# Router's first product in eight array tiles with two banks, and a first-layer product issued ahead of the turned result

## The reference, cut to what matters

```
h  = h + attention(layernorm(h))
x  = layernorm(h)                                   # 64 values a token
rh = relu(x @ router_w1 + router_b1)                # 64 -> 32
g  = softmax(rh @ router_w2 + router_b2)            # 32 -> 6, then the two best
h1 = relu(x @ expert_w1[e] + expert_b1[e])          # for each of the 6 experts
h2 = relu(h1 @ expert_w2[e] + expert_b2[e])
y  = sum over the two best e of weight_e * (h2 @ expert_w3[e] + expert_b3[e])
out = h + y
```

## Time and profile before

| | us |
|---|---|
| median of 3 runs | 247.37 |
| lowest, highest | 247.05, 250.84 |
| the profiled execution, as timed | 249.88 |
| its span in the trace | 248.1 |
| TensorE busy in it | 211.6 (85%) |
| VectorE busy | 159.6 (64%) |
| ScalarE busy | 106.6 (43%) |

### The profile page before, as it was taken

How to read it: one execution, slowest core, us unless ns; L and a number is a source line. 1 busy time by engine, 2 the same in 40 slices (tenths; PEclk the granted TensorE clock), 3 DMA queues, 4 the chain that set the end, 5 groups by cost and what they waited for, 6 DMA issues and landing times.

```text
span 248.1 us, 5974 instructions
## 1 busy us (share of the span) xinstructions
PE 211.6 (85%) x2394; PEld 88.3 (36%) x2398; DVE 159.6 (64%) x331; ACT 106.6 (43%) x188; POOL 77.8 (31%) x122
## 2 busy tenths in 40 slices
PE   0477876699899989998986889999999999998892
PEld 0354533034433433334542424434342523232210
DVE  3424673236795794798379498879889785928161
ACT  1228631123353353351245346555655555454530
POOL 4000465243352263303554307170625323201010
PEclk9999999569979988999999999999999999999997
DMA  7632399999698689710010669677663919384751
GB/s 144 147 121 53 81 223 239 262 264 260 178 260 209 174 225 262 194 68 18 3 42 4 168 154 213 137 161 162 164 156 103 210 53 242 77 215 104 180 132 42
DMA packets 26282, 37.85 MB, mean 153 GB/s; under 512 B 15888, under 2 KB 17104, under 8 KB 26256
## 3 DMA queue, kind: packets, MB, share of 16 engines
q1 hardware_dynamic: 19376, 19.92, 33.6%
q0 software_dynamic: 5216, 16.98, 26.4%
q10 hardware_dynamic: 1664, 0.58, 1.2%
HBM read 17.79 MB, written 2.83 MB: 83 GB/s over the span
## 4 chain that ended last, share of the span: by engine, by line
PE 60%; DVE 13%; DMA 9%; issue 9%; ACT 5%; POOL 2%; POOLq 1%; SPq 0%; DVEq 0%; ACTq 0%
PE PS L662 11%; PE PS L686 10%; PE PS L826 8%; PE PS L815 7%; PE PS L800 7%; DMA G<-Gs 5%; PE PS L746 3%; DVE Htab L954 2%; PE PS L698 2%; PE PS L837 2%; DMA WB<-gate_scratch 2%; ACT OT L566 2%; DMA cst<-consts 2%; PE PS L610 1%; PE PS L757 1%
## 5 line engine op out<-in xcount | busy, mean ns | idle before, releaser
L229 POOL DMA_DIRECT2D G<-Gs x64 | 33.6, 530 | 63.1 <-ACT Gs L472 56.8
L662 PE MATMUL PS<-A,BD 32*32 32x256 f32 x1024 | 35.8, 410 | 9.7 <-ACT Gs L472 6.4
L1071 DVE SCALAR_TENSOR_TENSOR H2g<-PS,nb_s,WB 128x1024 f32<-128x1024 f32 x24 | 30.8, 1283 | 13.6 <-PE PS L815 10.9
L488 ACT ACTIVATE H<-PS,b_s 128x512 f32<-128x512 f32 x48 | 30.2, 679 | 11.8 <-PE PS L800 11.8
L998 DVE COPY Gs<-PS 128x512 f32<-128x512 f32 x32 | 20.9, 686 | 21.0 <-PE PS L662 12.0
L686 PE MATMUL PS<-G,cnt 128*64 128x512 f32 x128 | 33.6, 662 | 0.0
L472 ACT ACTIVATE Gs<-PS 128x512 f32<-128x512 f32 x32 | 17.6, 595 | 33.3 <-PE PS L662 29.4
L400 POOL TENSOR_TENSOR GP<-GG,GP 32x512 fp32r<-32x512 f32 x8 | 10.2, 1269 | 66.2 <-ACT GP L504 66.2
L800 PE MATMUL PS<-X,W1s 64*128 64x512 f32 x96 | 27.1, 641 | 1.3 <-ACT H L488 1.3
L815 PE MATMUL PS<-H,W2s 64*64 64x512 f32 x192 | 26.1, 614 | 1.5 <-DVE H2g L1071 1.5
L826 PE MATMUL PS<-H2g,W3s 128*64 128x512 f32 x96 | 25.7, 616 | 0.9 <-DVE Y L1132 0.5
(11 more groups left out here) (114 smaller groups left out, 289.1 us busy)
## 6 DMA issues: line engine op xcount, KB each, us to landing
G<-Gs POOLq DMA_DIRECT2D x64, 256.0 KB, 6.5
WB<-gate_scratch SPq DMA_DIRECT2D x48, 256.0 KB, 5.3
xb<-ids_scratch SPq DMA_DIRECT2D x8, 256.0 KB, 3.8
h_out<-Y SPq DMA_DIRECT2D x8, 256.0 KB, 2.7
GG<-gate_scratch SPq DMA_DIRECT2D x64, 12.0 KB
vo_scratch<-VOs SPq DMA_DIRECT2D x2, 256.0 KB, 2.1
VOr<-vo_scratch SPq DMA_DIRECT2D x4, 128.0 KB, 3.1
wk_s<-wk SPq DMA_DIRECT2D x2, 128.0 KB, 5.0
```

What stands on the lines that cost most here:

```text
L229: eng.dma_start(G2[half % G2_RING][first::8, :, :], Gs[n % GS_RING][:, m, :]).then_inc(sent[n % GS_RING][m], 16)
L488: ins = act.activation(H1[q][:, u * HT:(u + 1) * HT], PS[:, B_L1 + u, :], ACT.Relu, bias=b1_s[:, u, q:q + 1])
L662: ins = pe.matmul(PS[32 * x:32 * x + 32, B_G + i, w * NV:(w + 1) * NV], BD[n % BD_RING][rows, x].rearrange("p c f -> p (c f)")[:, w::2], A ...
L1071: dve.scalar_tensor_tensor(out=H2g[q][:], in0=two_banks(l2_bank(q)), scalar=nb2_s[:, q:q + 1], in1=WB[s % RING][:, q, :], op0=ALU.max, op1 ...
```

## The change

Two things are changed. First, `hidden` makes its product in eight matmuls of 128 tokens in place of four of 256: one for each of the four 32-column groups and each of the two halves of partitions, the halves writing to the two banks `B_X` and `B_X + 1`. `hidden_out` reads both banks (as many values as before), and the order of the sequences that comes out makes the view in `rank_experts` a plain one.

```diff
                 for j in range(4):
-                    rows = slice(j // 2 * D, j // 2 * D + D)
-                    ins = pe.matmul(PS[32 * j:32 * j + 32, B_X + 1, 0:TOK // 4], R1[rows, :],
-                                    X2[i % RING][rows, j % 2 * (HT // 2):(j % 2 + 1) * (HT // 2)],
-                                    start=True, stop=True, skip_group_check=True)
+                    for u in range(2):
+                        rows = slice(u * D, (u + 1) * D)
+                        ins = pe.matmul(PS[32 * j:32 * j + 32, B_X + u, 0:S], R1[rows, :],
+                                        X2[i % RING][rows, j * S:(j + 1) * S],
+                                        start=True, stop=True, skip_group_check=True)
                 ins.then_inc(rh_ps, 1)
```

```diff
-                act.activation(RH[:], PS[:, B_X + 1, 0:TOK // 4], ACT.Relu, bias=rb1_s[:, 0:1]).then_inc(rh_sb, 1)
+                act.activation(RH[:].rearrange("p (u k) -> p u k", u=2), PS[:, B_X:B_X + 2, 0:S], ACT.Relu, bias=rb1_s[:, 0:1]).then_inc(rh_sb, 1)
```

```diff
-                then(dve.tensor_tensor(lg[:].rearrange("p (j c) e -> p j c e", c=2),
-                                       PS[:, B_X + 1, C_RL:C_RL + TB * E].rearrange("p (c j e) -> p j c e", c=2, e=E),
-                                       rb2_s[:].unsqueeze(1).unsqueeze(1).broadcast_to([P, TB // 2, 2, E]),
-                                       ALU.add), n + 1)
+                then(dve.tensor_tensor(lg[:], PS[:, B_X + 1, C_RL:C_RL + TB * E].rearrange("p (t e) -> p t e", e=E),
+                                       rb2_s[:].unsqueeze(1).broadcast_to([P, TB, E]), ALU.add), n + 1)
```

```diff
@@ TensorE's loop @@
                 if a:
                     router(i)
                 if b:
-                    layer1(s, 1)
                     layer2(s, 0)
...
                 if ahead:
                     hidden(i + 1)
+                if s + 1 < STEPS:
+                    layer1(s + 1, 1)
                 if b:
                     turn_out(s)
@@ ScalarE's loop @@
+                if b:
+                    relu1(s, 1)
                 if a:
                     act.wait_ge(rt_dve, RT * i + 4)
                     act.activation(ex[:], ex[:], ACT.Exp).then_inc(ex_act, 1)
-                if b:
-                    relu1(s, 1)
```

## The result

The changed kernel took 246.61 us (median of 20 runs, 243.05 to 250.42), the kernel before 247.61 beside it (20 runs, 246.20 to 250.84). The ratio is 0.9915, with a 95% interval of 0.9886 to 0.9944: 0.6 to 1.1% faster. The forecast was 247.1, within 245.6 to 249.0, and a gain of 0.26. The ratio compares only the executions within 1.5% of the fastest of each kernel, which are 10 of 20 here and 17 of 20 before, since one execution of the changed kernel was very short. All 20 against all 20, the medians differ by 1.0 and the means by 1.1. Two later timings gave 0.9966 [0.9920, 1.0011] and 0.9949 [0.9908, 0.9989]. So the change gives a little, about 1 us: by its middle value more than 0.26 in each of the three timings, though one interval takes in no change, and far from 2%.

What follows compares the result with a forecast made beforehand. TensorE's chain was taken to bound the kernel, with VectorE's path through Y to layer3(s, 0) deciding the change. Iterations 2 to 5 gain 1.04, 6 and 7 lose 0.78: -0.26, giving 247.1 us from 247.37, range 245.6 to 249.0.

Steps and rivals of the forecast that it cites:

- The mechanism: Mixture iterations: router 0.65 later delays VectorE, Y releases layer3(s, 0) at +7.20; 0.26 gained four times, 0.39 lost twice.
- The eight tiles: hidden on TensorE: two passes of 128 columns save 0.22, so it costs 0.35 for 0.57; bounds 0.57 and 0.30.
- The step that failed: TensorE's row behind hidden: router at +1.90, 0.49 after turn_out, and layer2(s, 0) 0.54 later at +2.44.
- The hidden values are not late either way: ScalarE's copy of the hidden values: done up to +1.18, with the router now at +1.90.
- Iteration 1, "nothing": Iteration 1: the moved product fills a 1.12 wait for RH, but the gain of about 1 is lost at the gates' DMA.
- Rival 1: hidden: the tiles save nothing, 0.57 stays; 0.04 saved four times, 0.61 lost twice, +1.1, 248.4 us; chance 0.15.
- Rival 2: VectorE doesn't bind after all: iterations 2 to 5 gain 0.41 each, 6 and 7 nothing; -1.6, 245.7 us; chance 0.08.
- Rival 3: TensorE's clock falls to half after a longer idle in iteration 1, 3.4 us at half costing 1.7; 248.8 us; chance 0.06.
- the 140 to 150 that was named as a sign: Changed profile: the forecast is wrong if the clock is below full between 140 and 150 us.
- The end: Behind turn_gates(7): the last L830 hangs on the gates' way through DRAM, so the end moves with the gates of step 7.

Runs made afterwards that it cites:

- early_with_gather: Changed kernel, but layer1(s, 1) goes ahead of turn_out only where the next iteration has a gather; 245.27 us, 0.9877 of the kernel before.
- result_first: Changed kernel with VectorE's result(s - 1), which makes Y, ahead of the ranks instead of behind two_best; 246.00 us, 0.9891 of the kernel before.
- order_only: Kernel before with layer1(s, 1) ahead of turn_out and its relu ahead of the exponential, hidden in the four old tiles; 249.22 us, 0.9965 of the kernel before.
- hidden_in_16: Changed kernel with each of the eight matmuls of hidden cut into two of 64 tokens; 249.68 us (1 run).
- both: Changed kernel with the edits of early_with_gather and result_first together; 246.74 us (median of 12 runs).

## Why the prediction was right or wrong

- **The mechanism** was right: the delayed router takes VectorE's ranks, `gate2` and `Y` with it, the hole moves from `OT` to `layer3(s, 0)`, the distance becomes the same with and without a gather, and the change gains in four iterations and loses in two. early_with_gather, result_first and order_only each hit this to 0.1 or better.
- **The eight tiles**: 0.35 was forecast, 0.38 measured; the second eight records start 0.13 behind the first, where 0.11 was taken for a pass. The Trainium skill's 25 ns (TensorE: Matmul & The Clock Gate, section "Wait — 56ns, not 53.3ns?") was rightly set aside for tiles side by side. The 0.38 alone wouldn't show it, since it is near the 0.40 that this rule gives as an estimate; the starts and hidden_in_16 do.
- **The step that failed** is a term of the sum: "`router` +1.90 (the 0.49 between them as before), `layer2(s, 0)` +2.44 (0.54)". The 0.54 of the router was taken over from the earlier trace rows, but it contained a weight load that had waited for `RH`. With `RH` early it is 0.45. That 0.09 less and the 0.03 more of `hidden` put `lg` at +2.49 for the forecast +2.54; `gate2` started 0.08 before the end of the ranks, where 0.05 was taken, at +4.32 for +4.40; and `layer3(s, 0)` came at +7.12 for +7.20: 0.08 in each of six iterations, 0.5. Measured is -0.34 four times and +0.31 twice, -0.7, where the sum had -0.26 four times and +0.39 twice. I had written "The hidden values are not late either way" and looked only at whether they arrive in time for the product, not for the load ahead of it. This makes the 0.7 of the stage; the rest of the timed 1 us isn't explained by any term, and that the time came out inside the range owes something to the range's width.
- **Iteration 1, "nothing"**: right at full clock to 0.1 (15.77 and 15.71 for 15.86). Wrong where the clock falls there by itself: then the moved product saves 1.0. The forecast knew the stretches only as a cost. In this profiled execution iteration 1 was 0.19 longer than before (16.05 for 15.86), since the one had a stretch and the other none.
- **Rival 1** (the tiles save nothing) is order_only: 0.4 slower in h2-g7, where 1.1 was forecast for it; the difference of 0.11 in each iteration is again the router's 0.08 and the 0.03 at `gate2`. **Rival 2** (VectorE doesn't bind) didn't come, but near: 0.12 is all that `Y` adds with a gather, where 0.15 was forecast. **Rival 3** came in one trace each of both and hidden_in_16, in the run both at its forecast price; none of the three traces of the changed kernel shows it. Their stretches begin ahead of the wait for the gates' DMA, in the same iteration, which here lies 5 us earlier than the 140 to 150 that was named as a sign.
- **The end** was right: from `turn_gates(7)` to the end 20.8 for 21.0.

## What to carry to other kernels

Moving a product of an in-order engine into a hole delays all that stands behind it: follow the delayed result through the other engine to the next point at which the first one waits, and do it for each kind of iteration, since the cover (here the gather) may be there in some only; then move it in those alone. When a duration is taken over from a row, ask whether it holds a weight load that was waiting for the same thing as the product. Where the whole time scatters more than the effect, read distances inside the stage: here those of an iteration repeat to 0.02 us when the time wanders by 5.

## What the runs showed of the hardware

- Eight tiles of 64x32 run side by side: sixteen records of 128 columns hold TensorE for 0.38, and 32 records of 64 columns also for 0.38, 0.012 apart in the mean.
- A product whose stationary operand is ready 0.1 earlier is itself shorter, 0.45 for 0.54 us for four records: its weight load starts 0.11 ahead of it, under the work in front, and not 0.02. The 0.45 is there in order_only too, with the old `hidden`.
- After a wait of TensorE of 2.54 and 2.65 us the clock fell to half for 3.4 us, after 1.47, 2.32 and 2.37 it did not. It also fell behind a wait of 1.56 and not behind another of 1.56 in the same trace, so these waits don't separate the two cases by their length.
